# Two slots in one: a new order of scores, weighing and turns in the wide layers, and the weighing of a batch in one run in the narrow ones

## The reference

```python
# for each layer
q = norm(x) @ wq;  k = ctx @ wk;  v = ctx @ wv        # split in 16 heads
q, k = rope(q), rope(k)                                # layer 2 only
scores = q @ k.T * scale                               # layer 2: -1e9 where the mask is off
attn = softmax(scores, axis=-1)
x = x + (attn @ v) @ wo                                # layer 2: layer norm of the sum behind it
```

## Time and profile before

| | us |
|---|---|
| median of 3 runs (lowest, highest) | 2117.78 (2115.46, 2123.31) |
| the profiled execution | 2111.77 |
| its span, first to last instruction | 2109.8 |

### The profile page before, as it was taken

One profiled execution on the slowest core, in us unless ns is written; L12 is line 12 of the kernel. 1 busy time (PEld: TensorE's weight loads), 2 busy tenths in 40 slices (PEclk: granted clock), 3 DMA queues, 4 the chain that ended last, 5 costly groups with the idle time before them and its releaser, 6 DMA issues. The chain is left out here.

```text
span 2109.8 us, 50608 instructions
## 1 busy us (share of the span) xinstructions
PE 1983.6 (94%) x18664; PEld 1642.0 (78%) x18664; DVE 1414.2 (67%) x2898; ACT 1276.3 (60%) x3249; POOL 562.3 (27%) x676
## 2 busy tenths in 40 slices
PE   7999996978999999999999999999999998899997
PEld 6777775977888888888777787877878876777786
DVE  4777875544545545555577887888788874677775
ACT  3777775545555555555556665666566653677775
POOL 3323320000000000000035755766666651000000
PEclk8999998999999999999999999999999998899999
DMA  5434442021000000000001000000000001344442
GB/s 165 154 125 139 145 131 101 7 73 38 16 8 9 15 9 8 15 9 8 16 1 51 10 15 11 9 10 17 9 10 10 9 1 34 108 131 131 124 124 70
DMA packets 72858, 109.63 MB, mean 52 GB/s; under 512 B 7052, under 2 KB 62508, under 8 KB 72620
## 3 DMA queue, kind: packets, MB, share of 16 engines
q1 hardware_dynamic: 72332, 105.88, 16.5%
q10 hardware_dynamic: 288, 0.51, 0.1%
HBM read 69.18 MB, written 37.19 MB: 50 GB/s over the span
## 5 line engine op out<-in xcount | busy, mean ns | idle before, releaser
L1516 ACT ACTIVATE wide_P<-PS,MX 100x361 f32<-100x361 f32 x512 | 288.3, 563 | 407.3 <-DVE MX L1634 407.3
L1634 DVE TENSOR_REDUCE MX<-PS 100x2 f32<-100x722 f32 x256 | 231.7, 905 | 148.0 <-PE PS L1386 146.5
L615 ACT ACTIVATE L_P<-PS,MX 100x361 f32<-100x361 f32 x512 | 252.7, 565 | 122.0 <-DVE MX L745 122.0
L745 DVE TENSOR_REDUCE MX<-PS 100x2 f32<-100x722 f32 x256 | 219.6, 899 | 45.2 <-PE PS L501 44.9
L1815 POOL TENSOR_TENSOR wide_AC<-wide_T,wide_COSM 128x362 f32<-128x362 f32 x128 | 130.1, 1016 | 336.3 <-ACT wide_T L1465 334.1
L513 PE MATMUL PP<-CON,L_P 100*128 100x100 f32 x1536 | 184.1, 257 | 26.4 <-DVE L_PT L752 17.5
L513 PEld LDWEIGHTS PP<-CON,L_P 100*128 100x128 f32 x1536 | 151.2, 144 | 48.4 <-ACT L_P L615 33.7
L1395 PE MATMUL PP<-CON,wide_P 100*128 100x100 f32 x1536 | 176.5, 251 | 0.0
L1395 PEld LDWEIGHTS PP<-CON,wide_P 100*128 100x128 f32 x1536 | 161.1, 142 | 9.0 <-issue 2.3
L1409 PE MATMUL PS<-wide_PT,wide_V 128*64 128x100 f32 (+1 forms) x3072 | 161.9, 254 | 0.0
L1409 PEld LDWEIGHTS PS<-wide_PT,wide_V 128*64 128x64 f32 (+1 forms) x3072 | 136.8, 137 | 31.0 <-issue 23.3
(11 more groups left out here) (242 smaller groups left out, 5355.2 us busy)
## 6 DMA issues: line engine op xcount, KB each, us to landing
strips<-L_KS SPq DMA_DIRECT2D x256, 90.5 KB
L_KA<-strips SPq DMA_DIRECT2D x64, 362.0 KB, 3.1
C<-ctx_t SPq DMA_DIRECT2D x32, 361.0 KB, 3.1
kept<-L_CTH SPq DMA_DIRECT2D x16, 361.0 KB, 4.7
kept<-L_CTL SPq DMA_DIRECT2D x16, 361.0 KB, 5.5
L_CTH<-kept SPq DMA_DIRECT2D x16, 361.0 KB, 4.2
L_CTL<-kept SPq DMA_DIRECT2D x16, 361.0 KB, 5.0
C<-in_ctx SPq DMA_DIRECT2D x8, 256.0 KB, 3.4
```

What stands on the lines that cost most here:

```text
L615: nc.scalar.activation(P[:, (4 * g + j) % 8, 0:SK], PSB[0:SQ, j, 0:SK], ACT.Exp, bias=MX[:, s % 2, 4 * q + j:4 * q + j + 1], scale=1.0).th ...
L745: nc.vector.tensor_reduce(MX[:, s % 2, 4 * q + 2 * i:4 * q + 2 * i + 2], PSB[0:SQ, 2 * i:2 * i + 2, 0:SK], AX.X, ALU.max, negate=True).the ...
L1516: nc.scalar.activation(P[:, (2 * g + i) % 4, 0:SK], PS_[i][0:SQ, 0:SK], ACT.Exp, bias=MX[:, s % 2, h:h + 1], scale=1.0, accum_out=DEN[:, s ...
L1634: nc.vector.tensor_reduce(MX[:, s % 2, 2 * p:2 * p + 2], PSB[0:SQ, 0:2, 0:SK], AX.X, ALU.max, negate=True).then_inc(Z["maxed"], 1)
```

## The change

**Wide layers.** A slot becomes a double slot d = 0 to 3 of two pairs (G = 4s + d; pairs 2G and 2G + 1). TensorE's order is: both scores, the weighing of both pairs of the double slot before, two K tiles (`first`), the turn of pair 2G, the jobs `mid`, the turn of pair 2G + 1, the jobs `late`. Turns thus stand in the double slot of their scores. Scores alternate between two sets of two banks, and a turn writes into the banks of its own scores; the banks that `PP` had go to the jobs and to the weighing. `PT` has four slots instead of six. Scores of a pair wait for the unloading two pairs back. Q tiles are spread: tiles 4 to 7 of the next pair of batches are made in the even batch, one in a double slot, tiles 0 to 3 in the odd one, so `QH` and `QL` have 12 slots. ScalarE makes four exponentials in a row ahead of all else. VectorE takes both maxima, then joins, then the shuffles of the new K tiles. The split of layer 2's Q weights is cut in two and begins in batch 13; x of the third and fourth batch is normalised and transposed in the prologue.

**Narrow layers.** In slot 1 the second half of the turn comes straight behind the scores, and the whole weighing behind it; ScalarE takes its result out behind the last exponentials.

```diff
 # narrow
-                        a_.append(("P1", s - 1, 0))
-                        b_.append(("P", s - 1, 0))
+                        a_.append(("P", s - 1, 0))
...
-                        for key in a_:
+                        turn_first = q == 1
+                        for key in [] if turn_first else a_:
                             job(key)
                         if 1 <= g <= NSLOT * B:
                             turn(g - 1, 1)
-                        for key in b_:
+                        for key in (a_ if turn_first else []) + b_:
                             job(key)
 # wide: banks and jobs
-            BANKS = [*PJ, PSB[:, 3, :]]
-            PO = PSB[:, 2, :]
+            BANKS = [*PJ, PP[1]]
+            PO = PP[0]
...
+            def jobs_at(s, d):
+                first, mid, late = [], [], []
                 if s + 1 < NS:
+                    first += [("K", s + 1, 2 * d), ("K", s + 1, 2 * d + 1)]
+                if s % 2 == 0 and s + 2 < NS:
+                    late.append(("Q", s + 2, 4 + d))
                 if s % 2 and s + 1 < NS:
+                    late.append(("Q", s + 1, d))
+                if s % 2 and d == 3 and s + 3 < NS:
+                    late.append(("X", s + 3, 0))
+                if d == 0 and s > 0:
+                    mid.append(("R", s - 1, 1))
+                if d == 0 and 0 < s < NS:
+                    mid.append(("V", s, 2))
+                if d == 1 and s > 0:
+                    mid.append(("O", s - 1, 0))
+                if d == 2 and s < NS:
+                    mid.append(("R", s, 0))
+                if d < 3 and s < NS:
+                    mid.append(("V", s, 3 + d))
+                if d >= 2 and s + 1 < NS:
+                    mid.append(("V", s + 1, d - 2))
+                return first, mid, late
...
+            def score_bank(g, i):
+                return PSB[:, 2 * (g % 2) + i, :]
 # wide: TensorE
-                        if g:
-                            pe.wait_ge(Z["exped"], 2 * g)
+                        if g >= 2:
+                            pe.wait_ge(Z["unloaded_even"], g - 1)
+                            pe.wait_ge(Z["unloaded_odd"], g - 1)
...
+                    for s, d in SLOTS:
+                        first, mid, late = jobs_at(s, d)
+                        G = 4 * s + d
                         if s < NS:
+                            scores(s, 2 * d)
+                            scores(s, 2 * d + 1)
+                        if 1 <= G <= 4 * NS:
+                            weigh(2 * G - 2)
+                            weigh(2 * G - 1)
+                        for key in first:
                             job(key)
+                        if s < NS:
+                            turn(2 * G)
+                        for key in mid:
                             job(key)
+                        if s < NS:
+                            turn(2 * G + 1)
+                        for key in late:
+                            job(key)
 # wide: VectorE
+                            maximum(2 * G)
+                            maximum(2 * G + 1)
+                        for key in turns_of(G - 1):
+                            join(key)
+                        if d == 0 and s:
+                            invert(s - 1, 1)
+                        if d == 2 and s < NS:
+                            invert(s, 0)
...
+                        for key in first:
+                            job(key)
+                        if s < NS:
+                            unload(2 * G)
+                        for key in turns_of(G - 1):
+                            rotated_low(key)
...
 # wide: chunks of layer 2's weights
-                      (1, "Q", 0, 1024), (1, "K", 0, 256), ...
-            CHUNKS_AT = {(14, 2): [5], (14, 7): [6], (15, 0): [7], (15, 1): [8, 9], (15, 2): [10], (15, 6): [11]}
+                      (1, "Q", 512, 1024), (1, "Q", 0, 512), (1, "K", 0, 256), ...
+            CHUNKS_AT = {(13, 0): [5], (14, 0): [6], (14, 3): [7], (15, 0): [8], (15, 1): [9, 10], (15, 2): [11], (15, 3): [12]}
```

More of the change, by code:

```diff
@@ L252, in narrow_layer @@
             PARTS = (0, 2, 1)
-            order = FIRST + [k for sl in SLOTS for part in jobs_at(*sl) for k in part if k[0] != "P1"]
+            order = FIRST + [k for sl in SLOTS for part in jobs_at(*sl) for k in part]
             job_no = {k: n for n, k in enumerate(order)}
@@ L440, in weigh @@
                         pe.wait_ge(Z["ones"], 1)
-                        pe.wait_ge(Z["unloaded_even"], NSLOT * s + 2 * half + 2)
-                        pe.wait_ge(Z["unloaded_odd"], NSLOT * s + 2 * half + 2)
-                        dst = begin(key) if half == 0 else bank(key)
-                        for q in (2 * half, 2 * half + 1):
+                        pe.wait_ge(Z["unloaded_even"], NSLOT * s + 4)
+                        pe.wait_ge(Z["unloaded_odd"], NSLOT * s + 4)
+                        dst = begin(key)
+                        for q in range(NSLOT):
                             for t, r in enumerate(KV_ROWS):
@@ L652, in _ @@
                             exponential(g, 3)
-                        for key in b_:
-                            job(key)
+                        for key in a_ + b_:
+                            if key[0] == "P" or key in b_:
+                                job(key)
                 @block.vector
@@ L1382, in scores @@
                             for n, r in halves:
-                                nc.tensor.matmul(PS_[n][0:SQ, 0:SKE], FILL[r, :], MNEG[r, v, :], start=True, stop=False)
+                                nc.tensor.matmul(score_bank(g, n)[0:SQ, 0:SKE], FILL[r, :], MNEG[r, v, :], start=True, stop=False)
                         for m, (Q_, K_) in enumerate(((QH, KH), (QH, KL), (QL, KH))):
                             for n, r in halves:
-                                last = nc.tensor.matmul(PS_[n][0:SQ, 0:SKE], Q_[r, p, q], K_[r, p, :], start=m == 0 and not rope(s), stop=m == 2)
+                                last = nc.tensor.matmul(score_bank(g, n)[0:SQ, 0:SKE], Q_[r, q_slot(s, p), q], K_[r, p, :], start=m == 0 and not rope(s), stop=m == 2)
                         last.then_inc(Z["scored"], 1)
@@ L1472, in rotated_high @@
                         hi, n, done = (KH, SKE, "k_high") if kind == "K" else (QH, 2 * SQ, "q_high")
-                        nc.scalar.activation(hi[:, p, :], AC[:, r % NB, 0:n], ACT.Copy).then_inc(Z[done], 1)
+                        nc.scalar.activation(hi[:, p if kind == "K" else q_slot(s, p), :], AC[:, r % NB, 0:n], ACT.Copy).then_inc(Z[done], 1)
                     def key_or_query(key, before):
@@ L1713, in _ @@
                     split_low(2)
+                    for v in range(2):
+                        x_stats(2, v)
+                    x_moments(2)
                     for p in range(HP):
@@ L1717, in _ @@
                     split_low(4)
-                    for key in FIRST[1 + HP:1 + 2 * HP]:
+                    x_norm(2)
+                    for key in FIRST[1 + HP:2 + 2 * HP]:
                         job(key)
@@ L1721, in _ @@
                         context_low(1, k)
-                    for s, p in SLOTS:
-                        after_scores, after_turn = jobs_at(s, p)
-                        g = HP * s + p
+                    for s, d in SLOTS:
+                        first, mid, late = jobs_at(s, d)
+                        G = 4 * s + d
                         if s < NS:
-                            maximum(g)
-                        shuffles_first = s + 1 < NS and rope(s + 1)
-                        if shuffles_first:
-                            for key in after_scores:
-                                job(key)
-                        if p == 2 and s:
+                            maximum(2 * G)
[6 more added lines that the diff above has]
+                            invert(s, 0)
+                        if d == 3 and s % 2 and s + 3 < B:
+                            x_norm(s + 3)
+                        for key in first:
+                            job(key)
+                        if s < NS:
+                            unload(2 * G)
+                        for key in turns_of(G - 1):
+                            rotated_low(key)
+                        if d == 1 and s + 2 < NS:
+                            for k in range(KE):
+                                context_low(s + 2, k)
+                        for key in mid:
+                            job(key)
+                        if s < NS:
+                            unload(2 * G + 1)
+                        if d == 0 and s:
@@ L1732, in _ @@
                             scale(s - 1, 1)
-                        if p == 6 and s < NS:
+                        if d == 2 and s < NS:
                             scale(s, 0)
-                        for key in turns_of(g - 1):
-                            join(key)
-                        if p == 0 and s:
-                            invert(s - 1, 1)
-                        if p == 4 and s < NS:
```

(5 more changed lines are left out.)

191 lines of the change are left out of this document (78 added, 113 removed).

## The result

The changed kernel takes 2086.96 us (median, 2085.16 to 2092.24) by 2119.99 of the kernel before on the same chip: 0.9869 of it, 95% interval 0.9841 to 0.9896. The medians differ by 33 us; the ratio gives 28, with 22 and 34 as ends. The terms of the forecast sum to a gain of 40 us, which gave 2078. The profiled execution took 2092.24 us, its span is 2090.4.

What follows compares the result with a forecast made beforehand. The prediction took TensorE's own stream to set the time in the 32 wide batches. Its terms, -42 + 5 - 5 - 2 + 1 + 3 = -40 us, gave 2078 us from the median 2117.8; the 8-in-10 range was 2048 to 2110.

Steps and rivals of the forecast that it cites:

- Shape changes, -42: Wide layers: fewer changes of TensorE's array shape save 0.33 us in each of 128 double slots, -42 us (-34 to -47).
- The cover of 0.2 in layer 1: Layer 1's V tile: its bank is free at 5.0 us, TensorE asks at 5.2 or later, so nothing waits.
- sign of being wrong: Forecast wrong if layer 1's V tiles wait for a bank, or the scores-to-weighing change costs more than 0.2 us.
- Rival 2: Slower, 2140 us: layer 1's K-tile bank is late too, with exponentials 0.75 us apart; chance 0.12.
- The waits of layer 2, +5: Layer 2: TensorE waits 1.5 us a batch against 1.2 before, over 16 batches, +5 us (-19 to +29).
- rival 1: VectorE sets layer 2, which gains nothing against 21 us of saved shape changes: 2094 to 2104 us; chance 0.14.
- Batch 14, -5: Batch 14: cutting the split of 1024 Q columns in two leaves 0.8 of a 5.5 us loss, -5 us (-5.5 to 0).
- the other chunks: The remaining weight-split chunks go together much as before: 0, give or take 2 us.
- Last batch -2: Last wide batch: eight waits of 0.34 us for exponentials become a few at the turns, -2 us (0 to -3).
- prologue +1: Prologue: a transpose job and some 1 us of VectorE work ahead of the first K tiles, +1 us (0 to +3).
- The narrow layers, +3: Narrow layers: 0.2 us of shape changes saved, 0.33 us of bare wait added, +3 us over 32 batches (-6 to +10).
- Periods: Batch periods expected in layer 1: near 35.3 and 40.4 us, with TensorE fully busy.

Runs made afterwards that it cites:

- split: The changed kernel with a double slot's two weighings moved between its two scores, same instructions: 2146.62 us, 1.0137 of the kernel before.
- q_late: New wide layers, old narrow ones, inversion ahead of joins, Q tile's join and high half behind K tiles' shuffles and copies: 2066.96 us, 0.9777 of the kernel before.

## Why the prediction was right, and by how much it was off

It forecast 2078 us, 1.9% less, and 2087 came, 1.3% less. The mechanism is the forecast's: fewer changes of shape pay, waits in layer 2 take some of it back. Two terms were too small, and in layer 1 two errors cancelled, which was luck.

**Shape changes, -42: the prices are right.** Scores to weighing costs 0.09, not up to 0.19, so the prediction's own sum was 0.37 a double slot, and not the 0.33 taken. Layer 1 gave 0.31, and with the 0.08 of waits for a bank added back 0.38. split is the second measurement: one change put back costs 0.17 in each double slot that doesn't wait, where the prices give 0.17. By the Trainium skill (TensorEngine Tiling (Array Packing), Key Properties) a change of mode drains the engine; priced by that alone two changes less were 0.18 a double slot and one more 0.09, and the traces have 0.31 to 0.38 and 0.17: the first matmul of the new shape holds 0.08 to 0.1 as well.

**The cover of 0.2 in layer 1: it failed in half of the places.** The prediction had the first maximum at 0.78 in every double slot, and so the bank free at 5.0 and no wait. In two of the four double slots of a pair in which a V tile follows the spread, VectorE has other work ahead of the maxima, and TensorE waits 0.17 and 0.45 us: 0.6 a pair, 5 us over the layer. So what the prediction itself named as a sign of being wrong did come, layer 1's V tiles wait for a bank; it was small. That layer 1 still came out near the mark (20 us for 21) is luck: the order gave 3 to 4 us more than the 0.33 says, and the waits took 5. Rival 2 had this place right but not its reason: the exponentials follow each other at 0.54 (1222.78, 1223.34, 1223.87), not 0.75. Its sum was also off: the other terms gain 45, not 50, which makes it 2145. In split, with the second scores 1.3 us later, a bank that is late in both layers is what happened.

**The waits of layer 2, +5: this is the step that failed in size.** By the subtraction of the prediction (the pair of layer 1 and 2.6 for the masks) they are 1.74 us a batch against 1.5 taken and 1.2 before; that is 4 us more over the layer, and the 0.31 for 0.33 is 1. The place was half right: the V tile waits 0.5 for the bank as said, but more is spent on R, ahead of it. I had put the inversion and its copy into VectorE's chain only to date the shuffle, and didn't ask who waits for the copy itself. Nor did I follow GpSimd: VectorE's join of a Q tile waits for it, and its multiplications lengthen VectorE's low halves by 0.3 to 0.6 us each. Batch 16 loses some 3 more (it and batch 17 take 84.79 us, 1.7 more than before): there the last weight chunk (1.22 us) stands ahead of VectorE's maxima, TensorE waits 0.3, 0.9 and 0.64 us within 3.5 us, and three matmuls later those of 512 columns run at half the clock, 0.63 instead of 0.39 us each:

```profile
1103.54 0.45 PE L1317 MATMUL PP<-wide_WH,wide_CTH 128*105 128x512 f32 x1 [0.64 <-ACT wide_T L1480]
1103.83 0.39 PE L1317 MATMUL PP<-wide_WL,wide_CTH 128*105 128x512 f32 x1
...
1104.72 0.63 PE L1317 MATMUL PP<-wide_WL,wide_CTH 128*105 128x512 f32 x1
```

Together layer 2 gave 5.9 us from its first batch to its last, where the terms (15 batches of 4 x 0.33, less 4.7) give 15. Of the 9 that are missing, 4, 1 and 3 are named; the one that is left over is a second stretch at half the clock, in another place in each profile: the first double slot of batch 30 takes 12.98 us in the first (11.45 in the second), that of batch 25 13.87 in the second (11.64 in the first).

**VectorE sets layer 2 (rival 1): no.** Its busy share rose from 77% and 88% to 90% in both batches, and yet moving its inversion and its last step of a batch, with nothing removed, took 20 us off layer 2 (618 to 597.4), at a share of 90% and 92%. Its order set the end, not its load. The prediction's reason against this rival was none, though: a stretch's busy time counts a moment once, however many spans cover it, so 88% was not overstated.

**Batch 14, -5: right.** It takes 38.46 us against 37.63 to 37.81 of its like (the even batches); 0.8 was left as said. Of the other chunks, priced at nothing, batch 15 gained 1.8 us more than its like (47.41 to 42.13, where odd batches went from 41.8 to 38.36), and batch 16 lost the 3 above. **Last batch -2, prologue +1:** layer 2's last batch to layer 3 gave 1.4 by two profiles each, and from the feed-forward to the first wide scores it took 113.5 and 117.0 us, where it was 112.1 and 111.8; the batch behind took 37.6 and 32.3, where it was 40.2 and 37.8. These are no larger than what two profiles of one kernel differ by, so I count them as not settled.

**The narrow layers, +3: 6.6 measured (3.4 to 9.7).** The wait was there and sized well (0.35 for 0.33), 0.15 a batch for 0.13. What was priced at nothing is the run of weighings at the end of each narrow layer, where no next batch hides it and the clock falls under it: by the profiles about 3.7 us at the end of layer 3 and 2.7 at that of layer 0. The parts add up to more than the 6.6, so that their shares are estimates.

**Periods.** I had said 35.3 and 40.4 us for layer 1; they are 37.64 and 38.42. The sum was right (75.7 forecast, 76.06 measured), by the luck told above; the parts ignored that the Q tiles are now spread over both.

## What to carry to other kernels

Price a change of TensorE's shape at two places, the last matmul of the old shape and the first of the new, and multiply: where TensorE is full that is the gain, less the waits that the new order makes. Look for these by the distance from start to start at the places that ask for a bank; a wait of 0.17 doesn't show as idle time. Then ask of every short product that TensorE reads (here RX) what stands ahead of it in its engine's order once the slot is longer; an inversion moved ahead of the joins and a layer norm step moved one double slot on were worth another 20 us, and the version with both and the old narrow order takes 2059.6 us against 2115.1 (with the late Q tile on top it is no slower, 0.9740 for 0.9744). Read the granted clock too before you price an order: waits of 1 to 2 us close together were at times followed by half the clock, for another 1.5 us. An order that is free in a steady loop is bare in the last batch of a layer: follow that one by itself.

## What the runs showed of the hardware

VectorE's low halves, which read two tiles of SBUF, took 1.6 to 2.7 times as long with GpSimd's full multiplications in the kernel (863 for 531 ns, 974 for 360), and its PSUM maximum the same 0.90; K tiles' low halves beside a single multiplication were not longer (524). A change of the array's shape cost TensorE 0.17 us, half in the last matmul of the old shape and half in the first of the new. Three waits of TensorE within 3.5 us, 1.8 us in all, were followed by a stretch at half the granted clock: seven matmuls started 0.43 us apart instead of 0.235, 1.4 us more. Waits of 1.4 and 0.3 us in q_late were followed by such a stretch in three batches and not in three others. And the same instructions with a pair of scores 1.3 us later were 57 us slower, of which the changes of shape that were added explain 22 (128 x 0.17) and the clock some 14.
